# One product in four moved to GpSimd, and decays from PSUM into SBUF, in the state loop of a fused Mamba and attention block

## What is computed

```python
Delta = softplus((h @ w_d1.T + b_d1) @ w_d2.T + b_d2)
A_bar = exp(-Delta[..., None] * A)                    # 16 states
BX = (Delta * h)[..., None] * Bm[:, :, None, :]
_, states = associative_scan(comb, (A_bar, BX), axis=1)
y = einsum('blfn,bln->blf', states, Cm) + D * h
```

## Time and profile before

| what | us |
|---|---|
| median of 3 runs | 2251.11 |
| lowest and highest of the 3 | 2248.17 to 2252.59 |
| the profiled execution, its own time | 2248.88 |
| span of its trace, first to last instruction | 2247.1 |
| outside the span | 1.78 |
| busy: PE, DVE, ACT, POOL | 1943.8, 1620.2, 1459.2, 948.8 |

### The profile page before, as it was taken

How to read it: one execution, slowest core, us unless ns; L and a number is a source line. 1 busy time by engine, 2 the same in 40 slices (tenths; PEclk the granted TensorE clock), 3 DMA queues, 4 the chain that set the end, 5 groups by cost and what they waited for, 6 DMA issues and landing times. The chain is left out here.

```text
span 2247.1 us, 33201 instructions
## 1 busy us (share of the span) xinstructions
PE 1943.8 (87%) x10218; PEld 1300.2 (58%) x10218; DVE 1620.2 (72%) x3001; ACT 1459.2 (65%) x2909; POOL 948.8 (42%) x909
## 2 busy tenths in 40 slices
PE   3759999889985999988988699998898679999798
PEld 1236676657524767665742567676574256676566
DVE  4867777658696777766768777775777877776587
ACT  2528777657652878765765477775675367777576
POOL 2555353234365443413436635341443564352243
PEclk9879999989987999998989799999998989999899
DMA  2001111001101111100110111110010011010011
GB/s 80 1 21 43 28 37 32 8 22 41 38 0 34 30 39 26 39 10 20 41 31 0 43 29 37 33 28 15 22 40 15 1 42 43 22 41 20 20 35 33
DMA packets 63328, 64.09 MB, mean 29 GB/s; under 512 B 12104, under 2 KB 46256, under 8 KB 63152
## 3 DMA queue, kind: packets, MB, share of 16 engines
q1 hardware_dynamic: 63152, 61.96, 10.5%
HBM read 26.26 MB, written 2.10 MB: 13 GB/s over the span
## 5 line engine op out<-in xcount | busy, mean ns | idle before, releaser
L787 ACT ACTIVATE probs<-ps,least 128x640 f32<-128x640 f32 (+7 forms) x512 | 380.6, 743 | 85.9 <-DVE least L1134 74.6
L799 ACT ACTIVATE probsT<-ps 128x512 f32<-128x512 f32 (+3 forms) x768 | 348.4, 491 | 120.3 <-PE ps L1504 111.9
L1504 PE MATMUL ps<-ident,probs 128*128 128x128 f32 x2304 | 349.2, 277 | 11.8 <-ACT probsT L799 4.5
L1494 PE MATMUL ps<-k_high,q_split 128*128 128x512 f32 (+3 forms) x768 | 303.6, 395 | 54.5 <-DVE q_split L1124 37.0
L1504 PEld LDWEIGHTS ps<-ident,probs 128*128 128x128 f32 x2304 | 271.3, 141 | 51.8 <-issue 22.6
L509 POOL TENSOR_SCALAR inverse_wide<-inverse 128x512 f32<-128x512 f32 x64 | 39.7, 621 | 545.8 <-DVE inverse L1145 545.8
L1141 DVE TENSOR_REDUCE least<-ps 128x1 f32<-128x640 f32 (+3 forms) x256 | 262.2, 1024 | 8.8
L1515 PE MATMUL ps<-probsT,vals 128*64 128x512 f32 (+3 forms) x1408 | 265.4, 498 | 0.4
L1495 PE MATMUL ps<-k_low,q_split 128*128 128x512 f32 (+3 forms) x768 | 261.5, 353 | 0.0
L1494 PEld LDWEIGHTS ps<-k_high,q_split 128*128 128x128 f32 x768 | 147.9, 193 | 177.6 <-ACT probs L787 85.7
L870 ACT ACTIVATE hid<-ps,cols 128x512 f32<-128x512 f32 x256 | 176.3, 689 | 112.6 <-PE ps L1341 112.2
(11 more groups left out here) (222 smaller groups left out, 3996.3 us busy)
## 6 DMA issues: line engine op xcount, KB each, us to landing
roped<-turned SPq DMA_DIRECT2D x512, 64.0 KB, 2.0
w<-in_w SPq DMA_DIRECT2D x128, 128.0 KB, 2.0
w_pair<-in_w_pairs SPq DMA_DIRECT2D x32, 128.0 KB, 2.6
xin<-in_x SPq DMA_DIRECT2D x4, 512.0 KB, 4.3
out<-acc SPq DMA_DIRECT2D x4, 512.0 KB, 3.2
pos<-in_c_pos SPq DMA_DIRECT2D x1, 512.0 KB, 4.7
v_w<-in_v_w SPq DMA_DIRECT2D x1, 512.0 KB
o_w<-in_o_w SPq DMA_DIRECT2D x1, 512.0 KB
```

The costliest lines, as they stand in the source:

```text
L787: act.activation(probs[:, t % 2, 0:width(t)], banks(2 * (t % 2))[:, 0:width(t)], ACT.Exp, bias=least[:, t:t + 1], scale=-1.0, accum_out=ro ...
L799: act.activation(dst, ps[:, T_BANK + g % 2, 0:k1 - k0], ACT.Copy).then_inc(t_taken, 1)
L1494: pe.matmul(o, q, k_high[par][h][:, k0:k1], start=True, stop=False)
L1504: made = pe.transpose(ps[:, T_BANK + g % 2, at - k0:at - k0 + P], probs[:, t % 2, at:at + P], ident[:, :])
```

## The change

The product of B for states 2, 6, 10 and 14 of each batch moves from DVE to POOL. POOL cannot read PSUM, so ACT first copies the broadcast row of B to a new SBUF tile `b_rows`. ACT writes all decays to two SBUF tiles in turn instead of PSUM banks 0 and 1. `bx`, `state` and `c_rows` become three tiles each instead of two, and the waits go one state further back. The orders become: ACT decay(i), C copy(i), and for i + 2 in the set the B copy(i + 2); POOL C product(i), and for i + 3 in the set the drive(i + 3), with drive(2) ahead of all; DVE as before with the four drives left out. PE's program is unchanged. A new semaphore `bx_pool` tells when a product on POOL is done; `bx_ready` is raised by DVE's drives and by the B copies.

```diff
+ON_POOL = (2, 6, 10, 14)
+DEEP = 3
...
+        decay = [sb(f"decay{i}", [P, SEQ], F32, e_ctx) for i in range(2)]
+        b_rows = sb("b_rows", [P, SEQ], F32, e_ctx)
...
+                def drive(i):
+                    n = b * STATES + i
+                    pool.wait_ge(bx_ready, n + 2)
+                    if n >= DEEP:
+                        pool.wait_ge(scanned, n - DEEP + 1 + 2)
+                    pool.tensor_tensor(bx[n % DEEP][:, :], du[:, :], b_rows[:, :], ALU.mult).then_inc(bx_pool, 1)
+
+                if 2 in ON_POOL:
+                    drive(2)
+                for i in range(STATES):
+                    n = b * STATES + i
+                    pool.wait_ge(c_taken, n + 2)
+                    pool.wait_ge(scanned, n + 3)
+
+                    pool.wait_ge(cs_used, n + 1)
+                    pool.tensor_tensor(cs[:, n % 2, :], state[n % DEEP][:, :], c_rows[n % DEEP][:, :], ALU.mult
+                                       ).then_inc(cs_ready, 1)
+                    if i + 3 in ON_POOL:
+                        drive(i + 3)
...
-                        act.wait_ge(scanned, n + 2)
-                        act.activation(banks(0), delta[:, :], ACT.Exp,
-                                       scale=neg_a[:, bass.ds(2 * r + k, 1)]).then_inc(decay_ready, 1)
...
+                    act.wait_ge(scanned, n + 1)
+                    act.activation(decay[n % 2][:, :], delta[:, :], ACT.Exp, scale=neg_a[:, i:i + 1]).then_inc(decay_ready, 1)
+                    act.wait_ge(c_bcast, n + 1)
+                    if n >= DEEP:
+                        act.wait_ge(cs_ready, n - DEEP + 1 + 2)
+                    act.activation(c_rows[n % DEEP][:, :], banks(4), ACT.Copy).then_inc(c_taken, 1)
+                    if i + 2 in ON_POOL:
+                        act.wait_ge(b_bcast, n + 3)
+                        made = ON_POOL.index(i + 2) + len(ON_POOL) * b
+                        if made:
+                            act.wait_ge(bx_pool, made)
+                        act.activation(b_rows[:, :], banks(2), ACT.Copy).then_inc(bx_ready, 1)
...
+                    if n >= DEEP:
+                        dve.wait_ge(scanned, n - DEEP + 1 + 2)
+                    dve.tensor_tensor(bx[n % DEEP][:, :], du[:, :], banks(2), ALU.mult).then_inc(bx_ready, 1)
...
+                    if i in ON_POOL:
+                        dve.wait_ge(bx_pool, ON_POOL.index(i) + 1 + len(ON_POOL) * b)
                     dve.wait_ge(decay_ready, n + 1)
...
+                    if n >= DEEP:
+                        dve.wait_ge(cs_ready, n - DEEP + 1 + 2)
+                    dve.sem_inc(passed, 1)
+                    dve.tensor_tensor_scan(state[n % DEEP][:, :], decay[n % 2][:, :], bx[n % DEEP][:, :], 0.0, ALU.mult, ALU.add
                                            ).then_inc(scanned, 1)
...
+                drive(0)
+                for i in range(STATES):
+                    if i + 1 < STATES and i + 1 not in ON_POOL:
+                        drive(i + 1)
+                    scan(i)
```

More of the change, by code:

```diff
@@ L224, in program @@
         du = sb("du", [P, SEQ], F32, m_ctx)
-        c_rows = sb("c_rows", [P, 2, SEQ], F32, m_ctx)
-        bx = sb("bx", [P, 2, SEQ], F32, m_ctx)
-        state = sb("state", [P, 2, SEQ], F32, m_ctx)
+        c_rows = [sb(f"c_rows{i}", [P, SEQ], F32, m_ctx) for i in range(2)]
+        bx = [sb(f"bx{i}", [P, SEQ], F32, m_ctx) for i in range(2)]
+        state = [sb(f"state{i}", [P, SEQ], F32, m_ctx) for i in range(2)]
         cs = sb("cs", [P, 2, SEQ], F32, m_ctx)
@@ L281, in program @@
         h_act = sb("h_act", [P, SEQ], F32, e_ctx)
+        c_rows.append(sb("c_rows2", [P, SEQ], F32, e_ctx))
+        bx.append(sb("bx2", [P, SEQ], F32, e_ctx))
+        state.append(sb("state2", [P, SEQ], F32, e_ctx))
+        decay = [sb(f"decay{i}", [P, SEQ], F32, e_ctx) for i in range(2)]
+        b_rows = sb("b_rows", [P, SEQ], F32, e_ctx)
         e_ctx.close()
@@ L320, in program @@
         b_bcast, c_bcast, c_taken = sem("b_bcast"), sem("c_bcast"), sem("c_taken")
+        bx_pool = sem("bx_pool")
         decay_ready, bx_ready, scanned, cs_ready, cs_used = (
@@ L759, in _ @@
                 act.sem_inc(passed, 1)
-                for r in range(0, STATES // 2):
-                    for k in range(2):
-                        n = b * STATES + 2 * r + k
-                        act.wait_ge(scanned, n + 2)
-                        act.activation(banks(0), delta[:, :], ACT.Exp,
-                                       scale=neg_a[:, bass.ds(2 * r + k, 1)]).then_inc(decay_ready, 1)
-                        act.wait_ge(c_bcast, n + 1)
-                        act.wait_ge(cs_ready, n + 1)
-                        act.activation(c_rows[:, k, :], banks(4), ACT.Copy).then_inc(c_taken, 1)
+                for i in range(STATES):
+                    n = b * STATES + i
+                    act.wait_ge(scanned, n + 1)
[10 more added lines that the diff above has]
+                        act.activation(b_rows[:, :], banks(2), ACT.Copy).then_inc(bx_ready, 1)
                 for c in range(2):
@@ L1038, in _, with drive, scan @@
                 dve.wait_ge(delta_ready, b + 1)
-                def drive(n, k):
+                def drive(i):
+                    n = b * STATES + i
                     dve.wait_ge(b_bcast, n + 1)
-                    dve.wait_ge(scanned, n + 1)
-                    dve.tensor_tensor(bx[:, k, :], du[:, :], banks(2), ALU.mult).then_inc(bx_ready, 1)
-                def scan(n, k):
+                    if n >= DEEP:
+                        dve.wait_ge(scanned, n - DEEP + 1 + 2)
+                    dve.tensor_tensor(bx[n % DEEP][:, :], du[:, :], banks(2), ALU.mult).then_inc(bx_ready, 1)
+                def scan(i):
+                    n = b * STATES + i
                     dve.wait_ge(bx_ready, n + 2)
+                    if i in ON_POOL:
+                        dve.wait_ge(bx_pool, ON_POOL.index(i) + 1 + len(ON_POOL) * b)
                     dve.wait_ge(decay_ready, n + 1)
-                    dve.wait_ge(cs_ready, n + 1)
-                    dve.tensor_tensor_scan(state[:, k, :], banks(0), bx[:, k, :], 0.0, ALU.mult, ALU.add
+                    if n >= DEEP:
+                        dve.wait_ge(cs_ready, n - DEEP + 1 + 2)
+                    dve.sem_inc(passed, 1)
+                    dve.tensor_tensor_scan(state[n % DEEP][:, :], decay[n % 2][:, :], bx[n % DEEP][:, :], 0.0, ALU.mult, ALU.add
                                            ).then_inc(scanned, 1)
[L1055 to L1063, removed]
+                drive(0)
+                for i in range(STATES):
+                    if i + 1 < STATES and i + 1 not in ON_POOL:
+                        drive(i + 1)
+                    scan(i)
                 dve.wait_ge(cs_used, STATES * b + STATES + 2)
```

## The result

The changed kernel takes 2337.8 us (median of 4 runs, 2334.55 to 2340.7), the kernel before 2251.85 (4 runs): ratio 1.0391, 95% interval 1.0372 to 1.0410. The ratio stands as the record gives it; the quotient of the two medians is 1.0382. The forecast was 2340 within 2325 to 2390.

A forecast was written before the change was run, and what follows sets the result against it. DVE set the pace at 3.53 us a state; afterwards DVE's and POOL's turns would: 32.4 + 44.4 + 0.8 + 2.1 = 79.7 us a batch against 57.52, 88.7 more in four, giving 2340 us, range 2325 to 2390.

The forecast's parts named there:

- Turns: State loop: a scan with two SBUF inputs and a POOL product exclude each other; waiting scan 2.16 us, product 2.22.
- The sum: First scan's end to gate product: 15 scans, 20 POOL products, extras, last add make 79.7 us against 57.52.
- The split: Over four loops, SBUF decays cost 67 us and the drives on POOL another 22.
- The loop with all drives on DVE: State loop with SBUF decays and no drives on POOL: 15 periods of 4.64 us, 74.2 us in all.
- the last add: PE's add at the loop's end, before the gate product: 0.10 + 1.94 us, with 0.04 to the gate, 2.1.
- No turn is lost to PE: State loop: B(k + 4) comes some 2.6 us after C product(k), well ahead of its drive, except once near the start.
- The pairs of products: At drives (6), (10), (14) and the last C product, two POOL products follow each other, each adding 0.20 us.
- The clock rival: State loop: TensorE falls to its lower clock, some 11.5 us more a batch, 46 in all, 2386 us; chance 0.17.
- The first rival: State loop: a scan takes no turns, between -3.3 and +0.9 us a batch, put at 2240 us; chance 0.10.

The follow-up runs named there:

- e4: The kernel before with one edit, the decay written to one SBUF tile instead of PSUM banks 0 and 1; 2326.18 us, ratio 1.0340.
- e5: The changed kernel with all drives on DVE and the C products left out, PE adding the states themselves; one execution, 2223.05 us.
- e1: The changed kernel with decays back in PSUM banks 0 and 1, four drives still on POOL; 2264.66 us, ratio 1.0082.
- e8: The changed kernel, all drives on DVE; even states: decay in PSUM, `bx` in SBUF; odd states the reverse; 2234.17 us, ratio 0.9923.
- e2: The changed kernel with all 16 drives on DVE, decays still in SBUF; 2321.05 us, ratio 1.0331.
- e3: The changed kernel with all drives on DVE and decays back in PSUM, leaving only the third tiles; 2257.52 us, ratio 1.0041.
- e6: The changed kernel with each pair of C broadcast matmuls on PE issued three times; 2343.24 us, ratio 1.0408.

## Why the prediction was right

- **Turns.** The step that carried the forecast, that a scan with two SBUF inputs takes turns with POOL's products, held. e4 shows it from one edit, e5 shows that it takes both engines, e1 and e8 show that one PSUM input ends it. No row before had a scan in such a pair; the rule of the Trainium skill (SBUF — State Buffer, section "SBUF: two separate sides"), that the pair of ports is held for a whole instruction, is what these runs show for the scan too, at 2.14 to 2.15 us from the turn's start to the scan's end (2.16 in the sum).
- **The sum.** 79.7 us a loop worked out, 79.2 measured; 88.7 us in all against 86.1. A POOL product that had waited cost 2.13 to 2.18 us, where the sum has 2.22.
- **The split** was off. It said 67 us for the decays and 22 for the drives on POOL. By the loops, e2 lies 70.9 above the kernel before (68.4 above e3, which has the third tiles too), and the changed kernel 15.3 above e2. The turns are not what was mis-sized. The loop with all drives on DVE is 74.2 in the text and 75.4 on average in e2. The term that was mis-sized is the last add: the text priced it at TensorE's upper level, and in e2 it ended 1.6 us later after the last product on average, which is all of the difference and some more. In the changed kernel it was not slowed. Counted from the first scan's end to the last product, the changed kernel's loops are 77.2 and e2's 71.8: 21.6 us in four, near the 22 of the text.
- **"No turn is lost to PE"** was true, but not for the reason given. The drive of 126.38 waited 2.58 us for its B broadcast, so that broadcast did not come well ahead. POOL had two products in hand by then and used the turns one behind the other (the three products of 117.27 end at 128.25); the scan got the next one. The pairs of products, each 0.20 in the sum, fell at this wait and not at the drives on POOL where the text put them. There are four in a loop either way, so the sum held, and in this it was lucky.
- **The clock rival** was half right: the granted clock fell to 0.80 in the loop, and the adds behind PE's long pause in each group began at the lower level (3.78 us at 121.70, 1.98 at 152.42 for the same four matmuls). The windows view of one group shows both levels:

```profile
119.60:126.42 6.82, 4.72 (x7) 1.78 (x8) 4.24 (x3) 1.05 (x1) 6.82 (x3) 0.50 0.00 0
126.42:140.08 13.66, 8.68 (x26) 3.20 (x24) 13.66 (x6) 8.72 (x9) 10.97 (x4) 1.00 0.00 0
```

  It did not cost what was priced, 11.5 us a loop, since PE rose to its upper level within the group and the waits fell into turns that POOL filled. In e2 and e4 it did cost, 1.6 us a loop at the last add. No run raised the clock in the changed kernel, so its own share there is not measured.
- **The first rival**, no turns for a scan, is excluded by e4 and the changed kernel's own records. Its price for the drives on POOL was also a little hopeful: e1, which runs without turns, lost 3.6 us a loop where it allowed from -3.3 to +0.9, though with one place for the decay and not two.

## What to carry to other kernels

Count the SBUF inputs of each VectorE instruction that runs beside GpSimd: moving one operand from PSUM to SBUF can cost more than the work it frees, though the instruction alone takes as long as before (the scan, 2.28 us in e5). Put one of the two inputs in PSUM, in place if need be, and the two engines run side by side, as scans of 2.26 to 2.29 us beside products of 2.36 in e1 and e8. Where a step leaves the engine that bounds a loop, look for the chain of equal length beside it (here scan, decay, scan) before counting on the gain.

## What the runs showed of the hardware beyond this

- A wait for a turn stands in the record's own duration and in busy time: POOL's busy time rose by 125.6 us, of which 16 products of 2.36 are 38.
- A scan with its decay in SBUF and its `bx` in PSUM takes 2.26 us and the reverse 2.29 (e8), 30 ns for the place alone.
- TensorE's granted clock was 0.80 to 0.81 in the changed kernel's loops, where PE pauses for 5.7 us in each group of four states, and 0.93 to 0.96 in those of the kernel before. More work alone did not raise it: e6, with 65 to 67 us busy in 81, was granted 0.80 to 0.85.
